# Message sums of a graph layer: scaling the one-hot masks by the edge attribute instead of the messages

## The reference

```python
mid0 = w_a * xg0 * ea0
mid1 = w_b * jnp.einsum('euc,ec->eu', xg1, ea1) * INV_SQRT3
mid2 = (w_c * xg0)[:, :, None] * ea1[:, None, :]
mid3 = (w_d * ea0)[:, :, None] * xg1
mids = jnp.concatenate([mid0, mid1, mid2.reshape(-1, 3 * MUL), mid3.reshape(-1, 3 * MUL)], axis=1)
agg = jax.ops.segment_sum(mids, edge_dst, num_segments=n)
```

## Time and profile before

| | us |
|---|---|
| median of 3 runs | 3106.43 (3104.78 to 3119.2) |
| span of the profiled execution | 3051.6 |
| message stage in it, from its first to its last operation | 1648 to 2476 |

### The profile page before, as it was taken

The page is one execution under the profiler, slowest core; times in us unless marked ns, Lnnn a source line. Parts: engine busy times, 40 slices in busy tenths (PEclk is TensorE's granted clock), DMA queues, the critical chain, the costliest instruction groups (busy, mean ns, idle before and its releaser), DMA issues. The chain is left out here.

```text
span 3051.6 us, 46067 instructions
## 1 busy us (share of the span) xinstructions
PE 2097.7 (69%) x9568; PEld 1514.9 (50%) x9568; DVE 1339.9 (44%) x3380; ACT 959.1 (31%) x3393; POOL 1149.8 (38%) x1193
## 2 busy tenths in 40 slices
PE   0145555656659753998034988989899878969991
PEld 0023333333336633998033665666666665538991
DVE  2522222222221450222553888888888862131112
ACT  0000000000004500222132766776677745413330
POOL 0056665656630034111702555555555510030004
PEclk9865565556559556999566999999999999969996
DMA  2223333333362015998311322322223310016553
GB/s 80 84 83 90 91 90 88 90 86 91 93 140 96 1 38 164 350 348 285 80 33 52 83 79 77 82 80 75 79 81 83 77 22 15 0 43 208 178 173 90
DMA packets 258620, 311.01 MB, mean 102 GB/s; under 512 B 108256, under 2 KB 200707, under 8 KB 258324
## 3 DMA queue, kind: packets, MB, share of 16 engines
q0 software_dynamic: 68352, 153.66, 18.2%
q1 hardware_dynamic: 189832, 154.07, 16.3%
q10 hardware_dynamic: 390, 2.76, 0.2%
HBM read 262.42 MB, written 47.78 MB: 102 GB/s over the span
## 5 line engine op out<-in xcount | busy, mean ns | idle before, releaser
L623 PE MATMUL sum_ps_sum<-sum_got,sum_onehot 128*125 128x256 f32 x928 | 429.0, 616 | 326.7 <-DMA sum_got<-xn_dram,sum_rec 165.7
L1751 POOL DMA_INDIRECT msg_got<-y_dram,msg_rec x464 | 456.5, 984 | 458.7 <-DMA msg_rec<-recs 303.0
L609 POOL DMA_INDIRECT sum_got<-xn_dram,sum_rec x464 | 447.5, 964 | 307.3 <-issue 158.1
L623 PEld LDWEIGHTS sum_ps_sum<-sum_got,sum_onehot 128*125 128x125 f32 x928 | 252.2, 299 | 503.3 <-issue 352.6
L1821 ACT ACTIVATE msg_part<-msg_got,msg_rec 128x64 f32<-128x64 f32 x1392 | 354.6, 332 | 2.6 <-DMA msg_got<-y_dram,msg_rec 2.5
L1773 PE MATMUL msg_ps_z<-msg_msg,msg_onehot_ea 128*125 128x256 f32 x928 | 265.4, 409 | 18.4 <-DVE msg_msg L1901 14.1
L1070 POOL DMA_INDIRECT ffn_rows<-xn_sb,ffn_slot_i x75 | 91.0, 1213 | 478.3 <-SPq L66 452.7
L1194 ACT ACTIVATE ffn_run_hid<-ffn_run_ps_h,cols 128x128 f32<-128x128 f32 x512 | 146.2, 369 | 379.8 <-PE ffn_run_ps_h L1143 379.8
L760 ACT ACTIVATE gin_h_t<-gin_ps_t 128x250 f32<-128x250 f32 x25 | 8.6, 379 | 793.7 <-PE gin_ps_t L815 793.7
L1143 PEld LDWEIGHTS ffn_run_ps_h<-ffn_run_rows_t,ffn_run_w 128*128 128x128 f32 x2048 | 248.1, 195 | 12.1 <-issue 4.8
L1143 PE MATMUL ffn_run_ps_h<-ffn_run_rows_t,ffn_run_w 128*128 128x128 f32 x2048 | 250.4, 279 | 4.0 <-DMA ffn_run_w<-in_L_ffn_w 1.7
(11 more groups left out here) (262 smaller groups left out, 2782.4 us busy)
## 6 DMA issues: line engine op xcount, KB each, us to landing
ffn_run_w<-in_L_ffn_w SPq DMA_DIRECT2D x128, 512.0 KB, 6.2
ffn_run_w<-in_L_ffn_Wd SPq DMA_DIRECT2D x32, 1024.0 KB
ffn_rows<-gin_zeros SPq DMA_DIRECT2D x24, 512.0 KB, 12.6
ffn_run_rows<-ffn_rows SPq DMA_DIRECT2D x96, 128.0 KB, 4.0
ffn_results<-ffn_run_res POOLq DMA_DIRECT2D x96, 128.0 KB
sum_got<-xn_dram,sum_rec POOLq DMA_INDIRECT x464
msg_got<-y_dram,msg_rec POOLq DMA_INDIRECT x464
sum_rec<-recs SPq DMA_DIRECT2D x232, 16.0 KB
```

What stands on the lines that cost most here:

```text
L609: pool.indirect_dma_start(got[s][u][:, :], None, k.xn_dram, bass.IndirectOffsetOnAxis(ap=rec[s][:, u, SRC:SRC + 1].bitcast(U32), axis=0)). ...
L623: last = pe.matmul(ps_sum[s][0:P, :], onehot[s][:, u, :], got[s][u][:, :], start=(u == 0), stop=(u == 1))
L1751: pool.indirect_dma_start(got[s][:, u, :, :].rearrange("p k v -> p (k v)"), None, k.y_dram, bass.IndirectOffsetOnAxis(ap=rec[s][:, u, SRC: ...
```

## The change

The three components of ea1 scale the mask instead of the message. VectorE makes onehot_ea0 itself, by a compare and a multiply in one operation for each u. ScalarE no longer makes part and instead makes onehot_ea1, three masks for each u. VectorE's msg has eight pieces: 0 to 3 as before, 4 to 6 are w_b * xg1 by component, 7 is w_c * xg0. TensorE sums, under the mask of component c, piece 4+c into column group 0 of the second half and piece 7 into group 1+c. The first call for the second half no longer carries start=True; the start of the half before it stands for both. The diff, without the declarations of tiles and semaphores (part, dot, part_made and msg_step go, onehot_ea1 and ea1_made come):

```diff
@@ -1768,11 +1767,20 @@
 
                 pe.wait_ge(ea0_made, 2 * n + 2)
                 pe.wait_ge(msg_made, n + 1)
-                for h, mask in enumerate((onehot_ea0[b], onehot[b])):
-                    for u in range(2):
-                        last = pe.matmul(ps_z[b][0:P, h, :], mask[:, u, :],
-                                         msg[b][:, u, 4 * h:4 * h + 4, :].rearrange("p k v -> p (k v)"),
-                                         start=(u == 0), stop=(u == 1))
+                for u in range(2):
+                    pe.matmul(ps_z[b][0:P, 0, :], onehot_ea0[b][:, u, :], msg[b][:, u, 0:4, :].rearrange("p k v -> p (k v)"),
+                              start=(u == 0), stop=False)
+                pe.wait_ge(ea1_made, 6 * n + 6)
+                sums = ps_z[b][0:P, 1, :].rearrange("p (k v) -> p k v", v=MUL)
+                for u in range(2):
+                    for c in range(3):
+                        mask = onehot_ea1[b][:, u, c, :]
+                        if u == 0 and c:
+                            pe.matmul(sums[:, 0, :], mask, msg[b][:, u, 4 + c, :], start=False, stop=False)
+                            pe.matmul(sums[:, 1 + c, :], mask, msg[b][:, u, 7, :], start=False, stop=False)
+                        else:
+                            last = pe.matmul(sums[:, 0:2 + c:1 + c, :], mask, msg[b][:, u, 4 + c:8:3 - c, :],
+                                             start=False, stop=(u == 1 and c == 2))
                 last.then_inc(summed, 1)
 
             def turn(i, first=False):
@@ -1809,46 +1817,33 @@
 
         @block.scalar
         def _(act):
-            def scale_parts(n, i, s, b, slot_used=True):
-
-                act.wait_ge(got_in[s % SLOTS], i * 32 + (32 if s >= 0 else 0))
-
-                if slot_used:
-                    act.wait_ge(msg_made, n - 1)
+            def scale_onehots(n, s, b, used=True):
+
+                act.wait_ge(masked, n + 1)
+                if used:
+                    act.wait_ge(summed, n - 1)
                 pass_on(act, gate)
                 for u in range(2):
                     for c in range(3):
-                        last = act.activation(part[b][:, u, c, :], got[s % SLOTS][:, u, 1 + c, :], ACT.Copy,
-                                              scale=rec[s % SLOTS][:, u, 9 + c:10 + c])
-                last.then_inc(part_made, 1)
-
-            def scale_onehots(n, s, b):
-
-                act.wait_ge(masked, n + 1)
-                pass_on(act, gate)
-                for u in range(2):
-                    act.activation(onehot_ea0[b][:, u, :], onehot[b][:, u, :], ACT.Copy, scale=rec[s % SLOTS][:, u, 8:9])\
-                       .then_inc(ea0_made, 1)
+                        act.activation(onehot_ea1[b][:, u, c, :], onehot[b][:, u, :], ACT.Copy, scale=rec[s % SLOTS][:, u, 9 + c:10 + c])\
+                           .then_inc(ea1_made, 1)
 
             def turn(i, first=False):
                 for s in range(SLOTS):
                     n, b = i * SLOTS + s, s % 2
                     act.wait_ge(attr_turned, n + 1)
                     act.activation(attr_t[b][:, :], ps_e[b][0:2 * REC, 0:128], ACT.Copy).then_inc(attr_kept, 1)
-                    if not first or s >= 1:
-                        scale_parts(n - 1, i, s - 1, 1 - b, slot_used=not first or s >= 3)
                     act.wait_ge(hid_sum, n + 1)
 
                     if not first or s >= 2:
                         act.wait_ge(w_sum, n - 1)
                     act.activation(hid[b][:, :], ps_e[b][:, 128:256], ACT.Silu, scale=1.0 / math.sqrt(8)).then_inc(hid_made, 1)
                     if not first or s >= 1:
-                        scale_onehots(n - 1, s - 1, 1 - b)
+                        scale_onehots(n - 1, s - 1, 1 - b, used=not first or s >= 3)
 
             turn(0, first=True)
             with act.Fori(1, turns) as i:
                 turn(i)
-            scale_parts(NEB - 1, turns - 1, SLOTS - 1, 1)
             scale_onehots(NEB - 1, SLOTS - 1, 1)
 
         @block.vector
@@ -1881,24 +1876,20 @@
                     if not first or s >= 2:
 
                         dve.wait_ge(summed, n - 1)
+                        dve.wait_ge(ea1_made, 6 * (n - 1))
                     dve.tensor_tensor(onehot[b][:, :, :], node_ids(k, tile), rec[s][:, :, DST:DST + 1].to_broadcast([128, 2, P]),
                                       ALU.is_equal).then_inc(masked, 1)
+                    for u in range(2):
+                        dve.tensor_scalar(onehot_ea0[b][:, u, :], k.iota[:, ds(tile * P, P)], rec[s][:, u, DST:DST + 1], rec[s][:, u, 8:9],
+                                          ALU.is_equal, ALU.mult).then_inc(ea0_made, 1)
                     w, y, m = ps_w[b], got[s], msg[b]
-                    ea1 = rec[s][:, :, 9:12].unsqueeze(3).to_broadcast([128, 2, 3, MUL])
                     dve.wait_ge(got_in[s], i * 32 + 32)
                     dve.wait_ge(w_sum, n + 1)
 
-                    dve.tensor_tensor(m[:, :, 0:9:8, :], w[:, :, 0:2, :], y[:, :, 0:1, :].to_broadcast([128, 2, 2, MUL]), ALU.mult)\
-                       .then_inc(msg_step, 1)
-                    dve.wait_ge(part_made, n + 1)
-                    pass_on(dve, gate)
-                    dve.tensor_reduce(dot[b][:, :, :], part[b][:, :, :, :].rearrange("p u c v -> p u v c"), AX.X, ALU.add)\
-                       .then_inc(msg_step, 1)
+                    dve.tensor_tensor(m[:, :, 0:8:7, :], w[:, :, 0:2, :], y[:, :, 0:1, :].to_broadcast([128, 2, 2, MUL]), ALU.mult)
                     dve.tensor_tensor(m[:, :, 1:4, :], w[:, :, 3:4, :].to_broadcast([128, 2, 3, MUL]), y[:, :, 1:4, :], ALU.mult)
-
-                    dve.wait_ge(msg_step, n * 2 + 2)
-                    dve.tensor_tensor(m[:, :, 5:8, :], m[:, :, 8:9, :].to_broadcast([128, 2, 3, MUL]), ea1, ALU.mult)
-                    dve.tensor_tensor(m[:, :, 4, :], w[:, :, 2, :], dot[b][:, :, :], ALU.mult).then_inc(msg_made, 1)
+                    dve.tensor_tensor(m[:, :, 4:7, :], w[:, :, 2:3, :].to_broadcast([128, 2, 3, MUL]), y[:, :, 1:4, :], ALU.mult)\
+                       .then_inc(msg_made, 1)
                     if not first or s >= 1:
                         add_sum(n - 1, 1 - b, tile_before, any_before=not first or s >= 2)
                     tile_before = tile
```

More of the change, by code:

```diff
@@ L1705, in sum_messages @@
         hid = [ph.sb(f"hid{b}", [128, 128]) for b in range(2)]
-        part = [ph.sb(f"part{b}", [128, 2, 3, MUL]) for b in range(2)]
-        dot = [ph.sb(f"dot{b}", [128, 2, MUL]) for b in range(2)]
-        msg = [ph.sb(f"msg{b}", [128, 2, 9, MUL]) for b in range(2)]
+        onehot_ea1 = [ph.sb(f"onehot_ea1{b}", [128, 2, 3, P]) for b in range(2)]
+        msg = [ph.sb(f"msg{b}", [128, 2, 8, MUL]) for b in range(2)]
         ps_e = [ph.ps(f"e{b}", [128, 512]) for b in range(2)]
@@ L1715, in sum_messages @@
             ph.sem(x) for x in ("attr_turned", "attr_kept", "hid_sum", "hid_made", "w_sum"))
-        ea0_made, part_made, masked, msg_step, msg_made, summed, added = (
-            ph.sem(x) for x in ("ea0_made", "part_made", "masked", "msg_step", "msg_made", "summed", "added"))
+        ea0_made, ea1_made, masked, msg_made, summed, added = (
+            ph.sem(x) for x in ("ea0_made", "ea1_made", "masked", "msg_made", "summed", "added"))
         fc1_zero, cleared, gate = ph.sem("fc1_zero"), ph.sem("cleared"), ph.sem("gate")
```

## The result

The kernel after takes 3201.35 us (median of 4, 3195.25 to 3213.44), the kernel before, timed beside it, 3112.81 us (median of 4, 3104.78 to 3124.26): a ratio of 1.0286, 95% interval 1.0242 to 1.0329.

What follows compares the result with a forecast made beforehand. TensorE was taken as the bound: 3.08 + 0.84 (sums) + 0.09 (wait) + 0.15 (idle) = 4.16 us a block, 155 us more over 232 blocks; span 3207 plus 54.8 gives 3262 us, range 3215 to 3370.

Steps and rivals of the forecast that it cites:

- the price of the new sums: TensorE, second half of the sums: 16 instructions with 16 weight loads take 1.71 us a block, 0.84 more than before.
- (a): TensorE sums: columns alone are the price, loads always hide; +0.43 us a block, 3167 us in all; chance 0.06.
- (b): TensorE sums: a load longer than the matmul before it isn't hidden at all; +1.27 us a block, 3361 us; chance 0.08.
- (d): TensorE sums: not slower, as same-mask calls need no new load or short pairs overlap; 3053 us; chance 0.03.
- ScalarE's six scales: ScalarE, message stage: six mask scales replace about 2.0 us a block, take 1.7 to 2.3, and end before the next transpose.
- (c): ScalarE becomes the bound: scales at 0.388 us each and late starts, 0.50 us idle a block; 3343 us; chance 0.06.
- VectorE's two compare-and-scale operations: VectorE, message stage: making the ea0 masks adds 0.2 to 0.6 us a block, against 0.71 removed.
- One sign: Profile after, message stage: VectorE's busy share was to be down by a quarter.
- around the span lie 54.8 us up to the median: Whole run: 54.8 us added to the forecast span of 3207 us to reach the median time, giving 3262 us.
- The extra wait: TensorE, between the ea0 group and the new sums: waiting for ea1_made costs 0.09 us a block, bounds 0 and 0.09.
- Idle time and slower starts: TensorE, message stage: of 0.41 us a block, 0.15 stays after the change, bounds 0.09 and 0.41.
- the 0.41 us a block of idle time: TensorE, kernel before: period of 3.49 us a block less 3.08 of work, taken as idle time or slower starts.

Runs made afterwards that it cites:

- f1: Kernel after, but pieces 4 to 7 summed by the old two calls under the plain mask; chip 0: 3073.5 us, ratio 1.000 to the kernel before.
- f5: Kernel after with the old two plain-mask calls for pieces 4 to 7, on chip 1: 2860.5 us, ratio 1.007 to the kernel before.
- b1: Kernel before, unchanged, profiled and timed again on chip 3: 2844.4 us in one run, message stage 740.7 us.
- b0: Kernel before, unchanged, profiled and timed again on chip 0: 3074.3 us, ratio 1.001, message stage 838.5 us.
- b3: Kernel before, unchanged, another profile on chip 0: 3062.5 us in one run, message stage 830.4 us.
- b4: Kernel before, unchanged, another profile on chip 1: 2840.5 us in one run, message stage 740.5 us.

## Why the prediction was right and wrong

**Right.** TensorE was the bound, and the price of the new sums: 1.71 us forecast, 1.75 measured. The eight 64-column instructions take 0.103 each (2211.09 to 2211.91), where I took 0.105; the 128-column ones 0.11 and 0.118, where I took 0.109. Half the columns save next to nothing, as they would if the load set the price; a fixed price of an instruction would look the same, for no run has 64 columns under a smaller load. Rivals (a) and (b) needed 0.054 and 0.159 and fell, and so did (d). The rule of the Trainium skill (TensorE: Matmul & The Clock Gate, "LDWEIGHTS (loading the stationary operand)") gives an estimate of 1.67 us for sixteen loads, and the trace's 1.75 agrees within 5%. ScalarE's six scales take 1.85 us (1.7 to 2.3 forecast) and end in time, so (c) fell. VectorE's two compare-and-scale operations take 0.51 us (0.2 to 0.6). That its relief is worth nothing fits f1 and f5, which change both engines at once; VectorE's part alone wasn't run. One sign came out smaller: VectorE's busy share of the stage fell from 84% to 69%, by less than a fifth and not by a quarter.

**The step that failed: "around the span lie 54.8 us up to the median".** A run's time is its span and under 2 us. The 54.8 us were the distance between a quick execution and the median of others. I carried them over to the kernel after as a constant, and it doesn't inherit them: its executions lie within 18 us in the first measurement, around 3201, and within 21 on chip 0. Without that term the forecast is 3053 + 155 = 3208 us. That this, like the forecast span of 3207 against 3211.7, is close is partly chance: the stage grew by 134 us and not 155, and 26 us came from outside it, 5 of them behind the stage and 21 because it starts later. It starts anywhere from 1648 to 1670 us in these traces and those from chip 0.

**Terms of the sum that were mis-sized.** The extra wait: 0.09 us forecast, nothing measured, as the ea0 group takes 0.96 us in both kernels and the first group behind the wait 0.22. Together with the sums' 0.04 the block is 3.96 us and not 4.01. Idle time and slower starts: 0.15 forecast. By the prediction's own measure, from the ea0 group of the second block to that of the last, the period is (2627.97 - 1694.55) / 230 = 4.06 us, so 0.10 above the block's 3.96; in steady work it is 4.2 us in 500, or 0.03 a block. The 0.05 of the block and the 0.05 of this term are 23 us over 232 blocks; the stage's growth of 134 us falls short of the 155 by 21. The long pause at the stage's start plays no part in it, as both kernels have it (8.12 us on TensorE before, 9.82 after).

**A premise that failed.** I took the 0.41 us a block of idle time for a property of the kernel, a hand-off "a little late". Some 0.08 of it is moreover TensorE's own work at the lower clock (738 us busy in the stage, where b1 has 720 for the same matmuls). On chips 1 and 3 the same program has 3.19 us a block (740.5 / 232), 0.11 above TensorE's stream. What a saturating change costs is its stream against the period of before, and that period is the chip's: 120 to 127 us on chip 0, 196 on chip 1, with the same terms. Why the first measurement has 88.5 us, less than any of these, stays open: its kernel before ran at 3105 to 3124 us, 50 to 70 above the execution that was profiled, and no profile shows where.

## What to carry over

Count instructions and their weight loads before columns when a sum is split over several masks: under a load of 125 columns an instruction took 0.10 to 0.12 us here with 64 columns and with 128, so that 4 loads turned into 16 doubled the sums' time (0.87 to 1.75 us) though the columns rose by half. Check what a profiled execution's own time is before taking its span for the median, and remember that a kernel saturated on one engine doesn't inherit the slack of the one before. Relief on an engine that isn't the bound gave nothing here, and the work moved to ScalarE stood in the way of a small copy that TensorE needs.

## What was not expected of the hardware

The same program takes 3070 us on chip 0 and 2841 to 2843 on chips 1, 3 and 13. Profile against profile (b0 and b3 against b1), 90 to 98 us of the difference are in the message stage and 133 to 144 ahead of it, and the part behind it is equal (576 to 581 us). Nearly all of what lies ahead is one loop, the destination sums of the first graph layer: VectorE's masks of it (L647) run from 170.8 to 903.2 us in b0 and from 170.5 to 763.2 in b1, 140 us longer. What differs in the message stage are pauses of up to 11.5 us on ScalarE for which the profile shows no awaited event. The granted clock has a share in it, behind the pauses: for the same 3480 matmuls TensorE is busy for 745 us of the stage in b0 and b3, at 0.97 and 0.96, and for 720 in b1, at 0.99. So some 25 us of the 90 to 98 are work that took longer, at the lower of the two levels (1.2 GHz) for part of it, and the other 65 to 73 are idle time. The Trainium skill (Runtime: NRT & Kernel Launch, "Instruction fetch mechanics") says that the refill of straight-line code is mostly hidden and that a taken branch to code outside the two pages at hand stalls for a fetch. VectorE's late start once a turn, 0.9 to 1.5 us, on chips 1 and 3 (b4, f5, b1) as on chip 0 (f1), does stand at the loop's jump; the long pause above stands in straight-line code. No run here shows whether either is an instruction fetch, nor what in chip 0 makes the difference.
